# A whole attention and feed-forward layer: quantisers thinned out before the first unit, half diagonal scores at other places, K evacuated by ScalarE, Q last, x rows ahead of up's weights

## The reference

```python
q, k, v = (x @ W.T + b, split into 16 heads of 64)
scores = einsum('bqhd,bkhd->bhqk', q, k) * 64 ** -0.5
scores = scores * exp(-alpha * abs(i - j))          # before the softmax
out    = einsum('bhqk,bkhd->bqhd', softmax(scores), v) @ Wo.T + bo
x1     = layernorm(x + out)
# fp4: blocks of 16, scale = max|.|/6, rounded to 0, .5, 1, 1.5, 2, 3, 4, 6
g, u   = fp4(x1) @ fp4(w_gate).T, fp4(x1) @ fp4(w_up).T        # 2816 wide
y      = layernorm(x1 + fp4(silu(g) * u) @ fp4(w_down).T)
```

## Time and profile before

| What | Value |
|---|---|
| runs, us | 1403.85, 1406.01, 1500.7; median 1406.01 |
| profiled execution, us | 1410.03; span of the slowest core (core 0) 1408.5, of the others 1391.1 to 1408.3 |
| TensorE busy | 1183.9 us, 84% of the span |
| VectorE busy | 1060.4 us, 75% |
| ScalarE busy | 707.0 us, 50% |
| GpSimd busy | 300.7 us, 21% |
| first jobs | to about 70 us |
| attention | to about 840 us, 32 units of 22.4 us in the middle |
| output projection and normalisation | about 805 to 931 us |
| feed-forward | about 927 to 1405 us |

### The profile page before, as it was taken

The page is one execution under the profiler, slowest core; times in us unless marked ns, Lnnn a source line. Parts: engine busy times, 40 slices in busy tenths (PEclk is TensorE's granted clock), DMA queues, the critical chain, the costliest instruction groups (busy, mean ns, idle before and its releaser), DMA issues.

```text
span 1408.5 us, 18014 instructions; the slowest of 8 cores (1391.1 to 1408.5 us)
## 1 busy us (share of the span) xinstructions
PE 1183.9 (84%) x5283; PEld 441.4 (31%) x5344; DVE 1060.4 (75%) x1360; ACT 707.0 (50%) x803; POOL 300.7 (21%) x513
## 2 busy tenths in 40 slices
PE   3959888888888888887886493899999999999993
PEld 1312222222222222222221131344444444444441
DVE  2778888888989887887897421549988888888870
ACT  1038767677777776777797343652211221122212
POOL 2002223232222232222322132420000110011001
PEclk9979999999999998999999696999999999999997
DMA  9564334344444533543446919683333242333321
GB/s 150 114 140 128 112 93 119 97 107 101 122 118 105 121 104 96 129 108 92 126 108 159 245 55 308 210 272 91 111 84 84 73 121 84 79 84 92 92 61 55
DMA packets 179315, 167.27 MB, mean 119 GB/s; under 512 B 141842, under 2 KB 141842, under 8 KB 178324
## 3 DMA queue, kind: packets, MB, share of 16 engines
q1 hardware_dynamic: 164132, 127.97, 34.1%
q0 software_dynamic: 15088, 38.16, 11.5%
HBM read 111.30 MB, written 34.34 MB: 103 GB/s over the span
## 4 chain that ended last, share of the span: by engine, by line
PE 45%; DVE 18%; issue 15%; DMA 11%; ACT 5%; POOL 3%; SPq 1%; DVEq 1%; POOLq 0%; ACTq 0%
PE ps L953 12%; PE ps L545 8%; PE ps L412 7%; PE ps L1022 6%; PE ps L466 4%; PE ps L485 4%; ACT PT L530 3%; DVE SD L498 3%; PE ps L407 3%; DMA den_scr<-AV 2%; DVE fr L232 2%; DMA cD<-den_scr 2%; DVE hb L237 2%; POOL stat L813 2%; DMA hb<-x 1%
## 5 line engine op out<-in xcount | busy, mean ns | idle before, releaser
L530 ACT ACTIVATE PT<-ps,tab 128x1024 bf16<-128x1024 f32 x384 | 410.0, 1117 | 115.4 <-PE ps L466 114.2
L545 PE MATMUL ps<-PT,V 128*128 128x512 bf16 x992 | 296.4, 392 | 6.9 <-issue 2.7
L466 PE MATMUL ps<-Q,KT 64*128 64x512 bf16 x768 | 180.6, 391 | 31.4 <-ACT PT L530 26.7
L485 PE MATMUL ps<-Q,KT 64*128 64x512 bf16 x256 | 100.1, 391 | 106.4 <-DVE SD L498 97.1
L498 DVE TENSOR_TENSOR SD<-ps,tab 128x512 f32<-128x512 f32 x256 | 174.0, 680 | 20.3 <-PE ps L485 13.9
L953 PE MATMUL ps<-wgT,x1qT 128*128 128x512 bf16 (+1 forms) x768 | 167.8, 362 | 3.5 <-ACT sg L963 3.0
L953 PE MATMUL ps<-wuT,x1qT 128*128 128x512 bf16 (+1 forms) x768 | 167.8, 362 | 0.0
L412 PE MATMUL ps<-xTs,wqk 128*128 128x512 bf16 x495 | 145.5, 408 | 24.9 <-DMA xTs<-xT 17.1
L1022 PE MATMUL ps<-wdT,hqT 128*128 128x512 bf16 x704 | 156.3, 382 | 2.7 <-DMA hqT<-hq 2.7
L530 ACT ACTIVATE PT<-SD 128x1024 bf16<-128x1024 f32 x128 | 135.6, 1059 | 7.7 <-DVE SD L498 7.5
L805 ACT ACTIVATE junk<-ring 128x1024 bf16<-128x1024 f32 x22 | 23.2, 1054 | 214.3 <-DVE ring L1030 205.1
(11 more groups left out here) (84 smaller groups left out, 1365.4 us busy)
## 6 DMA issues: line engine op xcount, KB each, us to landing
ring<-x_scr SPq DMA_DIRECT2D x32, 512.0 KB, 5.3
wst<-wg SPq DMA_DIRECT2D x22, 512.0 KB, 3.8
wst<-wu SPq DMA_DIRECT2D x22, 512.0 KB, 3.7
wst<-wd SPq DMA_DIRECT2D x16, 704.0 KB, 4.1
recD<-rec_scr POOLq DMA_DIRECT2D x64, 128.0 KB, 3.6
out<-ring POOLq DMA_DIRECT2D x16, 512.0 KB, 6.3
wg_scr<-wtr SPq DMA_DIRECT2D x22, 256.0 KB, 2.0
wu_scr<-wtr SPq DMA_DIRECT2D x22, 256.0 KB, 2.0
```

What stands on the lines that cost most here:

```text
L466: tok = op(TE, k0, lambda e, r0=r0, half=half: e.matmul(out=pt[:, half * 512:(half + 1) * 512], lhsT=KT[hp % 2][r0:r0 + 64, kt * 128:(kt + ...
L485: tok = op(TE, k0, lambda e: e.matmul(out=pt, lhsT=KT[hp % 2][r0:r0 + 64, kt * 128:(kt + 1) * 128], rhs=QR[u % 3][0][r0:r0 + 64, :], start ...
L530: f = op(AC, k0, lambda e: e.activation(out=PT[ri], in_=src, func=AF.Exp, scale=scl), [tok, pt_free[ri], t_tab])
L545: tok = op(TE, ka, lambda e, half=half: e.matmul(out=ps_ab[half], lhsT=VV[g][:, kt, hp % 4, 8 * half:8 * half + 128], rhs=PT[ri][:, half * ...
```

## The change

- Quantisation is laid over time with weights: 0.35 of the even density before unit 0, the full density in the units, and in the last unit only up to its third tile.
- The nominal times of the two diagonal halves are j - 4.985 and j - 2.985, where they were j - 4.4 and j - 2.8.
- K is evacuated by ScalarE, with its bias. Within units the evacuations of K and Q get a nominal time one tile later (Q had 0.6).
- The jobs of a unit come in the order V, K, Q.
- Buffers after the attention are laid out anew. `x1qT` comes first in its region, and the five slots of x rows 4 to 8 lie where quantisation had its buffers, so that these loads wait for quantisation alone and no more for `gate`.
- The loads of `wuT` stand behind later x rows on SP's queue: the first behind the load of row 12, the second behind the transposition of x1 row 0, the third behind the load of row 15, three more behind the transposition of x1 row 1. The quantisation of x1 rows 0 and 1 is started after rows 7 and 10, where it was 4 and 6. The first users of `hb` wait for `gate` and for the x row slots.

```diff
--- before.py
+++ after.py
@@ -193,16 +193,16 @@
         wuT = sb("wuT", NIT * D, BF16, O_R1 + 44 * KB).rearrange(
             "p (n c i) -> p n c i", c=NCT, i=128)
         O_Z = O_R1 + 88 * KB
-        hb = [sb(f"hb{i}", HF, F32, O_Z + 5632 * i) for i in range(3)]
-        hq = [sb(f"hq{i}", HF, BF16, O_Z + 16896 + 2816 * i) for i in range(2)]
-        hqT = [sb(f"hqT{i}", I_FF, BF16, O_Z + 22528 + 5632 * i).rearrange(
+        x1qT = [sb(f"x1qT{i}", D, BF16, O_Z + 2 * KB * i).rearrange(
+            "p (c t) -> p c t", t=128) for i in range(2)]
+        hb = [sb(f"hb{i}", HF, F32, O_Z + 4 * KB + 5632 * i) for i in range(3)]
+        hq = [sb(f"hq{i}", HF, BF16, O_Z + 20992 + 2816 * i) for i in range(2)]
+        hqT = [sb(f"hqT{i}", I_FF, BF16, O_Z + 26624 + 5632 * i).rearrange(
             "p (i t) -> p i t", t=128) for i in range(2)]
-        x1qT = [sb(f"x1qT{i}", D, BF16, O_Z + 33792 + 2 * KB * i).rearrange(
-            "p (c t) -> p c t", t=128) for i in range(2)]
-
-        wrow = [hb[0][:, 0:D], hb[1][:, 0:D], hb[2][:, 0:D],
-                sb("wrow4", D, F32, O_Z + 22528), sb("wrow5", D, F32, O_Z + 28160)] + ring
+
+        wrow = [sb(f"wrow{i}", D, F32, O_QZ + 4 * KB * i) for i in range(5)] + ring
         W_SLOT = [5, 6, 7, 8] + [(0, 1, 2, 3, 4, 5)[k % 6] for k in range(NTT - 4)]
+        assert O_QZ == O_Z + 15 * KB
         sg = [sb(f"sg{i}", QC, F32, O_C + 5 * KB + 2 * KB * i) for i in range(2)]
         x1q = [sb(f"x1q{i}", D, BF16, O_C + 9 * KB + 2 * KB * i) for i in range(2)]
         junk = sb("junk", D, BF16, O_C + 13 * KB)
@@ -367,9 +367,9 @@
                 vj = vj[1:]
             if u < 4:
                 continue
-            jobs[u] += [("Q", (u + 2) // 4, (u + 2) % 4)]
             if u // 4 + 1 < NP:
                 jobs[u].append(("K", u // 4 + 1, u % 4))
+            jobs[u].append(("Q", (u + 2) // 4, (u + 2) % 4))
 
 
 
@@ -423,13 +423,15 @@
                     op=ALU.add), [tok, t_b])
                 v_tok[(g, tt)] = f
             elif kind == "K":
-                f = op(DV, ke, lambda e: e.tensor_scalar(
-                    out=KT[hp % 2][:, c * 512:(c + 1) * 512], in0=pt,
-                    scalar1=bks[:, hp:hp + 1], scalar2=None, op0=ALU.add),
-                    [tok, t_c, slot_last.get(hp - 2)])
+                if bi == PB:
+                    ke += 1.0
+                f = op(AC, ke, lambda e: e.activation(
+                    out=KT[hp % 2][:, c * 512:(c + 1) * 512], in_=pt, func=AF.Identity,
+                    bias=bks[:, hp:hp + 1]), [tok, t_c, slot_last.get(hp - 2)])
                 k_tok[(hp, c)] = f
             else:
-                ke += 0.6
+                if bi == PB:
+                    ke += 1.0
                 qs_ = QR[(4 * hp + c) % 3]
                 old = q_last.get(4 * hp + c - 3)
                 f = op(AC, ke, lambda e: e.activation(
@@ -612,7 +614,7 @@
             for j in range(NTT):
                 if j % 4 == 3:
                     for half in range(2):
-                        seq.append((at(u, j - 4.4 + 1.6 * half), "D", (u, j, half), None))
+                        seq.append((at(u, (j - 4, j - 2)[half]) - 0.985, "D", (u, j, half), None))
                 else:
                     seq.append((at(u, j) - 0.98, "S", u, j))
             n = len(jobs[u])
@@ -653,17 +655,18 @@
                                                   wqo[0][:, 0:F], F, qr, qs))
                     for _, _, F in chunks)
 
-        spans = [(-30.0, at(0, 16))] + [(at(u, 1.9), at(u, 16.4)) for u in range(1, NU)]
-        spans[-1] = (spans[-1][0], at(NU - 1, 6))
-        room = sum(y - x for x, y in spans)
+        spans = ([(-30.0, 0.0, 0.35), (at(0, 0), at(0, 16), 1.0)]
+                 + [(at(u, 1.9), at(u, 16.4), 1.0) for u in range(1, NU - 1)]
+                 + [(at(NU - 1, 1.9), at(NU - 1, 3), 1.0)])
+        room = sum((y - x) * w for x, y, w in spans)
 
         def place(f):
 
             f *= room
-            for x, y in spans:
-                if f <= y - x:
-                    return x + f
-                f -= y - x
+            for x, y, w in spans:
+                if f <= (y - x) * w:
+                    return x + f / w
+                f -= (y - x) * w
             return spans[-1][1]
 
         done = 0.0
@@ -840,8 +843,8 @@
             else:
                 a = max(X0 - 8.0, pe[0] - 12.0,
                         w_free[s].at + 0.01 if w_free[s] else 0.0)
-                ld = fop(SP, a, lambda e: e.dma_start(out=row, in_=x_r[tt]),
-                         [w_free[s]] if w_free[s] else gate, sem=d_wl2[s], k=16)
+                ld = op(SP, a, lambda e: e.dma_start(out=row, in_=x_r[tt]),
+                        [w_free[s]] if w_free[s] else [prev] + t_ws, sem=d_wl2[s], k=16)
             y = y_n[0] % 2
             y_n[0] += 1
             t0 = max(pe[0], y_free[y][1] + 0.01, a + 0.1)
@@ -964,18 +967,18 @@
                 out=sg[g][:, 0:F], in_=ps_g[g][:, 0:F], func=AF.Silu), [tg, mo])
             silu_tok[n_] = si
             ch_ = h_chain[hs]
-            old = ch_.toks[4] if ch_ is not None else w_free[hs]
+            old = [ch_.toks[4]] if ch_ is not None else gate + list(w_free.values())
             mu, t = urgent(t0 + 0.05, 0.68 * F / 512, lambda e: e.tensor_tensor(
                 out=hb[hs][:, c0:c0 + F], in0=sg[g][:, 0:F], in1=ps_u[g][:, 0:F],
-                op=ALU.mult), [tk, si, old])
+                op=ALU.mult), [tk, si] + old)
             mul_tok[n_] = mu
             if ci % 3 == 2:
                 idx = 2 * tt + half
                 q = idx % 2
 
                 def done_(tok, t_):
-                    fr_ = d_last.get(tt - 2, w_free[3 + tt % 2] if tt < 2 else None)
-                    b_ = max(t_ + 0.05, fr_.at + 0.01)
+                    fr_ = d_last.get(tt - 2)
+                    b_ = max(t_ + 0.05, fr_.at + 0.01 if fr_ else 0.0)
                     hq_tr[idx] = fop(SP, b_, lambda e: e.dma_start_transpose(
                         out=hqT[tt % 2][:, 11 * half:11 * half + 11, :], in_=hq[q]),
                         [tok, fr_], sem=d_ht[half][tt % 2], k=16)
@@ -1037,17 +1040,18 @@
             out_last[s] = sv
 
 
-        for tt in range(4):
+        for tt in range(NTT):
             job_w(tt)
-        for c, (n0, nn) in enumerate(SEG):
-            t_wu[c] = op(SP, X0 - 7.0 + 0.1 * c, lambda e, n0=n0, nn=nn: e.dma_start(
-                out=flat(wuT[:, n0:n0 + nn]), in_=wus_r[:, n0:n0 + nn, :]),
-                gate, sem=d_wu[c], k=16)
-        for tt in range(4, NTT):
-            job_w(tt)
-            if tt == 4:
+            if tt >= 9 and tt % 2 or tt == 14:
+                c = (9, 11, 13, 14, 15).index(tt)
+                for c in ((c,), (c, c + 1))[tt == 15]:
+                    n0, nn = SEG[c]
+                    t_wu[c] = fop(SP, pe[0] - 2.0 + 0.1 * c, lambda e, n0=n0, nn=nn: e.dma_start(
+                        out=flat(wuT[:, n0:n0 + nn]), in_=wus_r[:, n0:n0 + nn, :]),
+                        gate, sem=d_wu[c], k=16)
+            if tt == 7:
                 start_x1(0, pe[0])
-            if tt == 6:
+            if tt == 10:
                 start_x1(1, pe[0])
         wd_s = wds_d.rearrange("q p x -> p q x")
         for h in range(2):
```

## The result

Over 20 runs each the changed kernel took 1418.9 us, the kernel before 1414.0; the ratio, formed from the undisturbed runs, is 1.0064 (95% interval 1.0035 to 1.0093). The forecast was 1367 us with a range of 1336 to 1397: neither time nor sign was right.

A forecast was written before the change was run, and what follows sets the result against it. TensorE and VectorE, each about 85% busy in attention, were taken to wait for each other; start -11, units -14 and tail -14 against 1410.0 gave 1371, less 4.0 for the median: 1367 us, range 1336 to 1397.

The forecast's parts named there:

- Start (-11): Before the first diagonal multiply: less quantiser work ahead of it and K off VectorE save 11 us.
- Units (-14): The attention units: K, quantiser, Q product and diagonal half terms together save 14 us.
- Diagonal halves +3: In the units: one more lone half each adds 6 us of TensorE work, half hidden, so 3 us lost.
- K's -19.5: In the units: 26 K evacuations leave VectorE, taking 19.5 us of its busy time away.
- -12 of the 23.9: In the units: half of VectorE's 23.9 us idleness before K goes; Q's products may take over the rest.
- rival D: In the units: ScalarE becomes the bound through waits before K and Q, making the kernel slower, 1471 us; chance 0.06.
- Tail (-14): Between attention and feed-forward: earlier x row loads bring the finals closer, less collision and slow clock costs; saves 14 us.
- +5 for the collision: In the last units: early x row loads slow one small normalisation hop on POOL's queue, costing 5 us.
- rival F: In the tail: small hops pass the large loads, so no collision cost; tail -19, 1362 us; chance 0.14.
- 62.3 instead of 83.0: In the tail: layer normalisation finals of rows 0 to 13 come 4.79 us apart, giving -20.7 us.
- E: Rival: the tail gives only -2, as x rows slow hops and up's weights come late; 1379 us; chance 0.07.
- B: Rival: in the units Q's products take over K's waits on VectorE, units give nothing; 1381 us; chance 0.20.

The follow-up runs named there:

- e4: The changed kernel with K evacuated by VectorE again; ratio to the kernel before 1.0084.
- e5: The changed kernel with the weight quantiser laid out as before, four chunks ahead of the first diagonal multiply; ratio to the kernel before 1.0082.
- e11: The kernel before with only the new places of the diagonal halves; ratio to the kernel before 1.0147.
- e13: The changed kernel with K back on VectorE and Q's job order and evacuation time as before; ratio to the kernel before 1.0255.
- e8: The changed kernel with the old job order (V, Q, K) and Q's old evacuation time, K still on ScalarE; ratio to the kernel before 1.0060.
- e9: The changed kernel with every K of the units evacuated twice by ScalarE; ratio to the kernel before 1.0157.
- e12: As e7, but x rows 4 to 8 are loaded only once the last normalisation is done; ratio to the kernel before 0.9893.
- e7: The changed kernel with the first hb product's wait narrowed and x1 rows 0, 1 and 2 read back earlier; ratio to the kernel before 0.9927.
- e3: The changed kernel with everything after the attention as before, so only start and units are changed; ratio to the kernel before 0.9958.
- e1: The changed kernel, but the first product into hb waits only for row slots sharing its memory; ratio to the kernel before 0.9992.

## Why the prediction was wrong

- **Start (-11).** Right in place and nearly in size: -8.3. Missing were the Q products' wait for ScalarE (1.50 us) and the 1.5 counted for K: with K back on VectorE (e4) unit 0 ends no later, at 102.6. TensorE's wait before the first SD was still 7.53 us, where some 3 were forecast. But the quantiser was counted as a loss of 14.8 in the units against this; it cost 8.6 there (e5), so this part of the change was worth nothing in the sum.
- **Units (-14): the first step that failed.** Of its terms, "Diagonal halves +3" was mis-sized most: alone they cost 20 us (e11). I counted TensorE's work in lone halves (0.19 us each) and not what the new places do to VectorE, which in e11 stands 38.3 us before its K instead of 22.8. K's -19.5 and the "-12 of the 23.9" together forecast -31.5, and TensorE's waits fell by 3 us. With the new places K's move brought 23 (e13 to e8), and the later Q brought 20 alone (e13 to e4). They do not add up: with either done, the other is free. What the moves repair is what the new places broke; with the quantiser's 8.6 that comes to about the +5 measured (20 - 23 + 8.6). So the forecast took three edits as independent terms that are one arrangement.
- **The cover of ScalarE's work.** It was named as "its 61.0 us of waiting for scores". e9 shows that this waiting covers little: 13 us lost for 18 us of work. So much of rival D holds; but K's waits stayed small, at 34 us in place of its 26 x 3.13 = 81.
- **Tail (-14): the second step that failed, and the larger.** The +5 for the collision was right (6 us, e12 against e7); in the first table it shows as 1.7 only, since the start and the units of the changed kernel alone (e3) shorten that stretch by 4.3, for a reason that no run isolates. The trace does not bear out that small hops pass freely beside the loads (rival F): 5.28 us against 1.69 for the same hop. The finals, "62.3 instead of 83.0", came to 73.7 on the mean: I had not followed SP's queue past the x rows, where x1 row 0's load now stands behind loads that wait for stores. And the diff's line that makes `hb` wait for every slot's last store was described, but never priced: 12.6 us of idle time. Without it (e1) 10 us come off.
- **The rule against additions on ScalarE** (the Trainium skill, ScalarE: Activation LUTs, Rules for kernel authors). Its figure is for bf16; here the source is float32 in PSUM, and the trace does not show the factor: K took 0.69 us on ScalarE, 0.75 on VectorE. Yet the move bought nothing (e4), as ScalarE has no room either (e9).
- **Rivals.** None named what happened. E had the tail give little, but at -2 and with up's weights late, which they were not (e1). B had the units give nothing, but not by its sign: Q's products on VectorE waited 6.3 us in all (core 3), not 0.9 each.

## What to carry to other kernels

Follow every queue to its end: a wait that is added "to be safe" is to be priced as the latest of all the things it names, here the store of the last row. In a loop where three engines are each busy 77 to 85% of the time, work moved between two of them is worth about nothing until a doubled copy of it shows a difference; price it that way first. And edits that move instructions past each other are one arrangement: undo them in pairs as well as singly, since each may be there for the other.

## What the runs showed of the chip

The granted clock of TensorE (a mean over stretches at its two levels, 2.4 and 1.2 GHz) differs from core to core in one execution, and the time goes with it: in the changed kernel's profile core 0 had 0.96 in the units and took 666.8 us, core 3 of the same die had 0.98 and took 649.2 and core 6 had 0.98 and took 646.2, with the same instructions. And small transfers (2 to 128 KB) are delayed by large loads on another queue: a hop of 4 KB took 5.28 us beside five loads of 0.5 MB and 1.69 without them, and the stretch of the last normalisations was 6 us shorter without them (e7 and e12).
